# Input projection of a Mamba layer: the integers of three later weights on GpSimd, the table steps divided anew among the stages

## The reference, cut to what matters

```python
def qa(x, s):  return jnp.clip(jnp.round(x / s), -128.0, 127.0)
def qw(w):     s = jnp.max(jnp.abs(w)) / 127.0; return (jnp.clip(jnp.round(w / s), -128.0, 127.0), s)
x_q = qa(hidden_states, S_IN)
wq, ws = qw(in_proj_w)
proj_q = qa(x_q @ wq.T * (S_IN * ws), S_Z)                 # 1024 channels hs, 1024 gate
conv_out = conv(hs_q, cwq) * (S_Z * cws) + conv_b          # causal, 4 taps, by channel
u_q = qa(jax.nn.silu(conv_out), S_U)
xwq, xws = qw(x_proj_w)                                    # x projection
dwq, dws = qw(dt_proj_w)                                   # step size, then softplus
ys = ssm_scan(u, dt, A, B_q * S_B, C_q * S_C)
owq, ows = qw(out_proj_w)                                  # output projection
```

## Time and profile before

| | us |
|---|---|
| median of 3 runs | 3638.93 |
| lowest and highest of them | 3637.65, 3646.35 |
| the profiled execution | 3631.06 |
| its span, first to last instruction | 3629.2 |
| TensorE, VectorE, ScalarE, GpSimd busy | 3210.9, 2432.7, 1772.8, 1209.1 |
| input projection | about 100 to 215 |
| x projection | about 215 to 262 |
| softplus | about 262 to 386 |

### The profile page before, as it was taken

One profiled execution on the slowest core, in us unless ns is written; L12 is line 12 of the kernel. 1 busy time (PEld: TensorE's weight loads), 2 busy tenths in 40 slices (PEclk: granted clock), 3 DMA queues, 4 the chain that ended last, 5 costly groups with the idle time before them and its releaser, 6 DMA issues. The chain is left out here.

```text
span 3629.2 us, 34786 instructions
## 1 busy us (share of the span) xinstructions
PE 3210.9 (88%) x11061; PEld 1573.1 (43%) x11061; DVE 2432.7 (67%) x4489; ACT 1772.8 (49%) x3342; POOL 1209.1 (33%) x963
## 2 busy tenths in 40 slices
PE   3750699999999799999999999899999978999963
PEld 3330244444444354554555555444444434444442
DVE  8769899999999555555555555543521156999854
ACT  4748466666666343434333343434410125888811
POOL 0433699999999001001000000022388020000024
PEclk9975799999999899999999999999999997999977
DMA  7125425343432312222211211234632011000046
GB/s 260 48 65 171 145 92 146 101 137 101 121 116 78 103 61 79 64 76 73 67 58 50 64 50 58 93 124 128 233 121 96 6 64 59 1 1 1 24 140 213
DMA packets 201317, 334.67 MB, mean 92 GB/s; under 512 B 25648, under 2 KB 76208, under 8 KB 198064
## 3 DMA queue, kind: packets, MB, share of 16 engines
q1 hardware_dynamic: 187904, 298.69, 25.4%
q0 software_dynamic: 12208, 33.57, 3.3%
q10 hardware_dynamic: 1024, 0.20, 0.0%
HBM read 217.69 MB, written 114.69 MB: 92 GB/s over the span
## 5 line engine op out<-in xcount | busy, mean ns | idle before, releaser
L1282 POOL TENSOR_TENSOR sc_dBu<-sc_dtu,xa 128x1024 f32<-128x1024 f32 x256 | 540.0, 2131 | 38.8 <-DMA sc_dtu<-scan_dtu 29.6
L1192 PE MATMUL y_ps<-sc_g,ident 128*128 128x512 f32 x1024 | 476.2, 600 | 18.6 <-POOL sc_g L1270 12.1
L1306 DVE TENSOR_TENSOR_SCAN sc_dA<-sc_dA,sc_dBu 128x1024 f32<-128x1024 f32 x160 | 365.1, 2282 | 6.9 <-POOL sc_dBu L1282 6.9
L1565 ACT ACTIVATE c_p<-c_ps,c_sm 128x512 f32<-128x512 f32 x256 | 195.5, 774 | 354.5 <-DVE c_sm L1606 354.5
L1605 DVE TENSOR_REDUCE c_sm<-c_ps 128x4 f32<-128x2048 f32 x64 | 146.7, 2292 | 312.7 <-PE c_ps L1528 312.7
L1246 ACT ACTIVATE sc_dA<-sc_dt,a_neg 128x511 f32<-128x511 f32 x512 | 329.6, 676 | 11.2 <-DVE sc_g L1306 9.8
L1192 PEld LDWEIGHTS y_ps<-sc_g,ident 128*128 128x128 f32 x1024 | 189.8, 190 | 256.6 <-issue 168.1
L1598 DVE SCALAR_TENSOR_TENSOR xa<-c_ps,c_sm,xa 128x512 f32<-128x512 f32 x256 | 192.2, 751 | 147.0 <-PE c_ps L1518 133.3
L1518 PE MATMUL c_ps<-c_wo,c_oT 128*128 128x512 f32 x512 | 246.5, 605 | 2.3 <-DVE xa L1598 1.6
L1499 PE MATMUL c_ps<-u,c_wq 128*128 128x512 f32 x512 | 233.1, 598 | 4.5 <-DMA c_wq<-in_c_wq_dram 4.5
L1547 PE MATMUL c_ps<-c_pT,c_v 128*128 128x512 f32 x512 | 230.8, 593 | 2.1 <-DVE c_pT L1617 2.0
(11 more groups left out here) (538 smaller groups left out, 6104.5 us busy)
## 6 DMA issues: line engine op xcount, KB each, us to landing
kv_w<-in_c_wkv_dram SPq DMA_DIRECT2D x32, 512.0 KB, 4.1
cross_keys<-kv_out SPq DMA_DIRECT2D x64, 256.0 KB, 2.0
cross_values<-kv_out SPq DMA_DIRECT2D x128, 128.0 KB, 1.9
c_kT<-cross_keys SPq DMA_DIRECT2D x64, 256.0 KB, 2.7
c_rk<-cross_rk SPq DMA_DIRECT2D x64, 256.0 KB, 3.4
c_v<-cross_values SPq DMA_DIRECT2D x64, 256.0 KB, 2.7
expert_rows<-e_yt SPq DMA_DIRECT2D x63, 256.0 KB, 2.0
xa<-scan_bc SPq DMA_DIRECT2D x48, 256.0 KB, 8.4
```

The costliest lines, as they stand in the source:

```text
L1192: ins = pe.matmul(yps[:, k % 2, :], ident[:], g[:, c % GS, n, :], start=False, stop=(m == NCH - 1 and n == NG - 1))
L1282: pool.tensor_tensor(dBu[:, c % 3], spread(dtu[:, k % DT, :], NG), bc[:, m * NG:(m + 1) * NG, :], ALU.mult).then_inc(s_dBu, 1)
L1306: dve.tensor_tensor_scan(to.rearrange("p n s -> p (n s)"), dA[:, c % 2].rearrange("p n s -> p (n s)"), dBu[:, c % 3].rearrange("p n s -> p ...
L1565: ins = act.activation(pr[:, j, :], ps[:, SB + j, :], ACT.Exp, scale=rq[:, j:j + 1], bias=bias[:, j:j + 1], accum_out=l[:, j:j + 1])
```

## The change

The two passes of each of the four integers move from ScalarE's program to GpSimd's, where they stand ahead of the table steps, as tensor_scalars. The semaphores are the same ones. Of the table steps now 9 instead of 14 are in the input projection, 6 as before in the x projection, and 17 instead of 12 in softplus.

```diff
-CELL_STEPS = (14, 20, ST)
+CELL_STEPS = (9, 15, ST)
...
             @block.gpsimd
             def _(pool):
                 pool.memset(hs[:, :, :, 0:PAD], 0.0).then_inc(s_pad, 1)
+                pool.wait_ge(s_inv, 1)
+                for i, (w, r, n, _) in enumerate(chunks):
+                    if i == 2:
+                        pool.wait_ge(s_q, 1)
+                    pool.tensor_scalar(n, r, winv[:, w:w + 1], MAGIC, ALU.mult, ALU.add).then_inc(s_near, 1)
+                    pool.wait_ge(s_near, i + 1)
+                    pool.tensor_scalar(n, n, MAGIC, None, ALU.subtract).then_inc(s_int, 1)
                 add_cells(pool, rmw, s_sum, 0, CELL_STEPS[0])
...
-                def integer(i):
-                    w, r, n, _ = chunks[i]
-                    if i == 0:
-                        act.wait_ge(s_inv, 1)
-                    if i == 2:
-                        act.wait_ge(s_q, 1)
-                    act.activation(n, r, ACT.Copy, scale=winv[:, w:w + 1], bias=MAGIC).then_inc(s_near, 1)
-                    act.wait_ge(s_near, i + 1)
-                    act.activation(n, n, ACT.Copy, bias=-MAGIC).then_inc(s_int, 1)
-
...
-                    if k in (1, 3, 6, 13):
-                        integer((1, 3, 6, 13).index(k))
```

## The result

| | before | after |
|---|---|---|
| median of 8 runs, us | 3642.64 (3634.96 to 3649.89) | 3656.05 (3651.95 to 3660.93) |
| after / before | | 1.0036, 95% interval 1.0024 to 1.0049 |
| profiled execution, us (span) | 3631.06 (3629.2) | 3660.93 (3658.9) |

The change costs 13.4 us on the medians, where the forecast said 12.4, for which it named two places and one relief. The interval reaches from 1.0024 to 1.0049, so the loss is clear of no change and lies between 9 and 18 us. The two profiled executions lie 29.7 us apart: the one of before was faster than any of its eight timed runs, the one of after the slowest of its eight.

What follows compares the result with a forecast made beforehand. ScalarE and VectorE were taken to lead the input projection by turns, its last store ending it, as in softplus. -4.6 + 7.5 + 9.5 = +12.4 us on a median of 3638.93 gave 3651, range 3640 to 3666.

Steps and rivals of the forecast that it cites:

- two places and one relief: Passes holding up VectorE in the input projection, +7.5 us; extra table steps in softplus, +9.5; ScalarE's lighter load, -4.6.
- the scan's start near 399: Sign after softplus: GpSimd's last scatter issued near 396 us, the scan starting near 399 instead of 386.4.
- the store of the last Silu at 212: Sign at the input projection's end: the last Silu's store at about 212 us; before, it was issued at 209.10.
- GpSimd's 13 us of passes: Sign in the input projection: eight GpSimd tensor_scalars with 13 us of work, single ones stretched by up to 2.35.
- ScalarE's relief, -4.6: Input projection: activations leaving ScalarE save 2.4 us of VectorE's standing still and 2.2 us for the last pair.
- The length of a pass: GpSimd in the input projection: sized by the affine select, 1.32, 2.01, 2.01 and 1.09 us a pass, 12.9 for eight.
- The second rival: Input projection: passes cost as much as a tensor_tensor, 4.3 us each; sum +26 us, 3665; chance 0.13.
- What the passes take from VectorE, +7.5: Input projection: GpSimd and VectorE take turns; first four passes cost 1.3 us beyond idle time, other four 6.2.
- The nine steps, hidden with 4 us to spare: Input projection: nine table steps from about 145 us end at 212, while the stage ends at 216.
- Softplus, +9.5: Softplus: 17 table steps instead of 12 end at 394.8 us, against 385.35 for the last store.
- The first rival: Input projection: passes run beside VectorE at no cost to it; sum +4.9 us, 3644; chance 0.2.
- The third: Input projection: TensorE's 15.3 us of waits for ScalarE vanish, softplus steps at their cheapest; -10 us, 3629; chance 0.07.

Runs made afterwards that it cites:

- e_before: The kernel before, unedited, run again for a second profile: ratio 1.0006 (0.9996 to 1.0016) to before, input projection 115.9 us.
- e_after: The changed kernel, unedited, run again: ratio 1.0044 (1.0031 to 1.0057) to before, input projection 124.2 us, softplus 136.0.
- e_noint: The kernel before without the eight ScalarE activations for the later weights' integers, nothing in their place, values meaningless: ratio 0.9988 (0.9979 to 0.9997).
- e_price: The kernel before plus a measuring section after the input projection, with GpSimd passes alone and beside VectorE work: timed once, 3765.54 us.
- e_muladd: The changed kernel with each second pass written as multiply and add instead of one subtraction: ratio 1.0038 (1.0024 to 1.0052) to before.
- e_divide: The changed kernel with multiply-and-add second passes and table steps divided 10, 8, 14 instead of 9, 6, 17: ratio 1.0009 (1.0000 to 1.0018) to before.
- e_steps: The kernel before with only the table steps divided 9, 6, 17 instead of 14, 6, 12, integers left on ScalarE: ratio 1.0031 (1.0020 to 1.0043).

## Why the prediction was right, and where its terms were off

The sign, the size (13.4 us for 12.4) and the two places were right, and the range of 3640 to 3666 held the time. That the size came so near is luck in part. The input projection and softplus together lost 19.6 us by the profiles of e_before and e_after, and the scan started 20.8 us later (24.1 in the first pair), for 12.4 forecast; a stage that the forecast did not name gave 5.8 back. Of its signs, the scan's start near 399 was 408.7 to 410.5, the store of the last Silu at 212 was 219.5, and GpSimd's 13 us of passes were 29.3 with their waits. The terms, by the stages of e_before and e_after:

- **ScalarE's relief, -4.6.** Right as far as the runs show: 0.9988 in time, or 4.4 us (1 to 8). The last Silu's store came 6.2 us earlier in e_noint, so the relief may be 1.6 us larger where no table step ends the stage.
- **The length of a pass.** The first passes took 1.97 us at 2048 columns for 2.01 forecast. The second were sized by the affine select too, as the same shape, and this step failed: they take 5.4 us with VectorE quiet. By the prices of e_price all eight are 1.3 + 2 x 2.0 + 1.1 = 6.4 for the first and 3.4 + 2 x 5.4 + 2.8 = 17.0 for the second (1280 columns scaled), 23.4 us where 12.9 stood. The second rival had the price of a tensor_tensor for all eight, 26.6 us in all. That total is near, but by luck: its passes of 4.3 us at 2048 columns are neither 2.0 nor 5.4, and its stage (+16.7) was too long.
- **What the passes take from VectorE, +7.5.** The turns are shown. The stage's net is +8.3 for the 2.9 forecast. With passes of the forecast's length (e_muladd) it is -1.0 or -0.2 instead of +2.9: relief and turns together were 3 to 4 us too dear for passes of that length. VectorE's busy time rose by 7.9 us there and the stage by nothing, so VectorE had more waits to absorb the turns than its two stretches said; up to 1.6 us of it can be the larger relief. Too short a pass and too dear a turn covered each other in part. The page of the Trainium skill that the forecast weighed (GPSIMD Engine Reference, Elementwise — side-by-side cycle accounting) was near for multiply and add, 1.15 cycles at 1.2 GHz an element by these rows for its 1.03 (0.98 by the step from 1024 to 2048 columns), and far off for a single subtraction, 3.2 cycles.
- **The nine steps, hidden with 4 us to spare.** They began at 154.60 instead of 145 and took 68.5 us for 67. Their last scatter's issue ends at 223.08 and the x projection starts 2.7 us behind it, the time that e_divide shows where the steps alone end the stage; the last store, issued at 219.52, is followed by the same start after 6.2 us, for 6.1 before, where the store ended it. So both end together: hidden, but with nothing to spare, and so late only because the stage itself had grown. In e_muladd, with short passes, they began at 143.01 and ended at 212.77, as forecast (212). The stage ended 2.7 us behind that and 6.2 behind the last store at 209.20: there too both end together. The forecast left out the tail of 2.7 us and had the store at 212.
- **Softplus, +9.5.** +11.3 in e_after, +11.2 in e_steps, +13.6 in the first profile. With five steps more the issue of the last scatter ends 30.9 us (e_after, e_steps) to 33.2 us (after) later in the stage, for 31.6 forecast. That is partly chance: in e_after the last five took 34.0 us and the first twelve 3.1 us less than in e_before. What was too small is the tail: from the end of the last scatter's issue to the scan 5.0 us, where 1.4 + 1.0 stood. These 2.6 us, less the 0.7 by which 30.9 falls short of 31.6, are within rounding the 1.8 us by which e_after exceeds the forecast.
- **The forecast had no term for heads,** -5.8, which made the total fit again. Its cause is open.

The first rival (passes that cost nothing, 3644) was wrong, since VectorE does stand; even with fast passes the stage, at -0.2 to -1.0 us in e_muladd, is as far from its -4.6 as from the forecast's +2.9. The third, TensorE running through, did not happen: its waits for ScalarE grew from 13.0 or 15.3 to 20.1 us.

## What to carry to other kernels

Before work is given to GpSimd, price each form of it, not each shape: the same columns cost 0.96, 2.6 or 3.5 ns each by the pair of operations, and n - MAGIC written as n * 1.0 + (-MAGIC) took 8.7 us out of a stage. Beside VectorE's tensor_scalar or scalar_tensor_tensor a pass costs VectorE its whole length, so put it where VectorE waits. When a chain of dependent transfers is moved into a stage with slack, count how many links the slack holds; the rest is paid in full, and the tail from the last issue to the barrier belongs into the sum. And hold a forecast against each stage: a total that fits can hide terms that don't.

## What the runs showed that was not expected

- GpSimd's tensor_scalar on FP32, 2048 columns: multiply and add 1.96 us, one operation 5.37 to 5.45, subtract and add 7.10, a tensor_tensor 4.49. More operations can be cheaper than fewer.
- A tensor_scalar of VectorE over 128 BF16 columns, 0.2 us alone, took 2.45 us on the mean beside GpSimd's passes, and a scalar_tensor_tensor over 2048 columns 3.8 us; a tensor_reduce over 2048 columns was not held up (2286 ns).
- TensorE's granted clock fell to its lower level in stretches behind waits of some 4 us in some executions and not in others of the same kernel (before at 130 to 150 us: 1.00; e_before at 140 to 150: 0.66), and 16 matmuls took 6.29 instead of 3.64 us for it. With one profile of a stage this can't be told from an effect of 4 us.
- Two executions of one kernel differed by 15.4 us in the first experts, with 274 instead of 326 GB/s in one stretch.
